# Attention in a hybrid block: sixteen small folds and divisions per launch replaced by four large ones

## The reference, cut to what matters

```python
scores = jnp.einsum('bhqd,bhkd->bhqk', q, k) * SCALE + add_mask
attn = jax.nn.softmax(scores, axis=-1)
out = jnp.einsum('bhqk,bhkd->bhqd', attn, v)
out = out.transpose(0, 2, 1, 3).reshape(b, n, H * HD)
return out @ Wo.T + bo
```

## Time and profile before

| | |
|---|---|
| time, median of 3 runs | 570.11 us (568.11 to 571.6) |
| profiled execution, first to last instruction (the page has no other time for it) | 597.5 us |
| attention loop in the profiled execution (first to last weighing) | 43.7 to 219.6 us |
| busy: PE, DVE, ACT, POOL | 82%, 72%, 56%, 44% of the span |
| 128x64 products of `weighed_T` | 128 records, 19.3 us together |

### The profile page before, as it was taken

One profiled execution on the slowest core, in us unless ns is written; L12 is line 12 of the kernel. 1 busy time (PEld: TensorE's weight loads), 2 busy tenths in 40 slices (PEclk: granted clock), 3 DMA queues, 4 the chain that ended last, 5 costly groups with the idle time before them and its releaser, 6 DMA issues.

```text
span 597.5 us, 14116 instructions
## 1 busy us (share of the span) xinstructions
PE 488.9 (82%) x4941; PEld 319.0 (53%) x4943; DVE 431.1 (72%) x1154; ACT 332.1 (56%) x509; POOL 265.0 (44%) x242
## 2 busy tenths in 40 slices
PE   7778879986999878689998887779989958879840
PEld 2435447554656545335687775225555536768730
DVE  5658896787898977566387774798988753767746
ACT  1337556554778752546377774246857823757730
POOL 5409970027000033776155556383356760645550
PEclk9999998997999998788998999978999978989985
DMA  4893642442432380111478661999001015786616
GB/s 121 203 414 88 167 111 57 123 111 67 109 98 55 101 248 2 41 50 45 130 236 251 199 194 42 238 181 150 20 19 35 29 45 157 214 251 192 187 42 210
DMA packets 85738, 78.16 MB, mean 131 GB/s; under 512 B 9645, under 2 KB 72518, under 8 KB 85286
## 3 DMA queue, kind: packets, MB, share of 16 engines
q1 hardware_dynamic: 76208, 57.81, 38.0%
q0 software_dynamic: 4544, 9.38, 4.6%
q10 hardware_dynamic: 4918, 10.07, 4.6%
HBM read 39.92 MB, written 30.88 MB: 119 GB/s over the span
## 4 chain that ended last, share of the span: by engine, by line
PE 45%; DVE 24%; ACT 9%; another core or an unknown queue 7%; issue 6%; DMA 5%; POOL 2%; SPq 2%; DVEq 0%; ACTq 0%; POOLq 0%
PE ps L1608 6%; DVE max_words L1870 5%; PE ps L1622 4%; PE ps L1361 4%; PE ps L1482 3%; PE ps L1336 3%; PE ps L1373 3%; PE ps L1285 2%; PE ps L1623 2%; ACT arena L1149 2%; ACT probs L948 2%; PE ps L1305 2%; PE ps L1559 2%; DMA arena<-y_dram 2%
## 5 line engine op out<-in xcount | busy, mean ns | idle before, releaser
L876 POOL DMA_INDIRECT y_dram<-arena,goes_to x78 | 83.5, 1071 | 91.8 <-DVE goes_to L2119 69.8
L1870 DVE TENSOR_REDUCE max_words<-ps 128x2 f32<-128x256 f32 (+3 forms) x128 | 98.6, 818 | 28.3 <-PE ps L1310 28.1
L948 ACT ACTIVATE probs<-ps 128x768 f32<-128x768 f32 (+1 forms) x96 | 81.1, 881 | 44.7 <-PE ps L1341 44.5
L727 POOL TENSOR_TENSOR rstd<-var_eps,minus_half 128x4 f32<-128x4 f32 x16 | 17.5, 1091 | 144.4 <-DVE var_eps L1837 144.4
L1149 ACT ACTIVATE arena<-ps,up_back 128x512 f32<-128x512 f32 x78 | 53.0, 679 | 48.7 <-PE ps L1608 23.3
L867 POOL DMA_INDIRECT rows_dram<-probs,idx x64 | 66.0, 1031 | 27.6 <-issue 18.0
L1608 PE MATMUL ps<-arena 128*128 128x128 f16 x936 | 65.9, 221 | 11.4 <-DVE arena L2125 11.4
L1622 PE MATMUL ps<-w,probs 128*128 x312 | 62.3, 278 | 14.3 <-DVE probs L2131 10.4
L2131 DVE SCALAR_TENSOR_TENSOR probs<-arena,hid_scale,probs 128x512 f16<-128x512 f32 x78 | 58.3, 747 | 12.8 <-ACT probs L1154 8.5
L1608 PEld LDWEIGHTS ps<-arena 128*128 128x128 f16 x936 | 56.1, 99 | 14.0 <-issue 13.7
L1482 PE MATMUL ps<-w,ident_f 128*128 128x512 f16 x184 | 53.1, 406 | 10.0 <-ACT arena L1105 3.4
(11 more groups left out here) (231 smaller groups left out, 1006.8 us busy)
## 6 DMA issues: line engine op xcount, KB each, us to landing
arena<-weights_dram SPq DMA_DIRECT2D x78, 256.0 KB
rows_dram<-grids SPq DMA_DIRECT2D x64, 260.0 KB, 4.4
heads_arena<-q_words SPq DMA_DIRECT2D x45, 128.0 KB, 2.5
qk_sb<-rows_dram SPq DMA_DIRECT2D x78, 65.0 KB
arena<-in_w ACTq DMA_DIRECT2D x2, 2304.0 KB
weights_dram<-w SPq DMA_DIRECT2D x2, 1152.0 KB, 8.4
w<-in_last_w ACTq DMA_DIRECT2D x1, 2048.0 KB, 19.2
arena<-y_dram SPq DMA_DIRECT2D x16, 128.0 KB, 4.5
```

Of the source, the lines that this page charges most:

```text
L876: nc.gpsimd.indirect_dma_start(y_dram.ap(), bass.IndirectOffsetOnAxis(ap=goes_to[:, n % AT_GO:n % AT_GO + 1], axis=0), y_t[:, n % YT, :], ...
L948: nc.scalar.activation(probs[:, n % 2, :, PROB_AT[u]:PROB_AT[u] + size], ps[:, of:of + 2, 0:size], ACT.Exp).then_inc(slot_free[slot_of(("T ...
L1870: ins = nc.vector.tensor_reduce(max_words[:, n % 2, :, t], ps[:, of:of + 2, o:o + keys], AX.X, ALU.max)
```

## The change

`weighed` gets four copies, one per quad of a batch (`weighed_of`, on words of other tiles that are idle then), so PE no longer folds each quad. Once per batch `fold_values` multiplies all four at once: `fold` is now the stationary operand, 32 columns wide, and the four quads go to the four groups of 32 columns of the array and so to the four quarters of the partitions. It does so twice, once for the numerators (first bank of the slot `at`) and once for the sums, repeated eight times so that they stand under the numerators (second bank). The result already stands as features by tokens. DVE's `divide` is called once per batch: a reciprocal of 128x512 and a product of 128x512 straight into `attT`; DVE now frees the slot `at`. The transposes, ACT's copy, `att` and the semaphores `sums_full` and `sums_free` go away. The order of the eight banks in `RINGS["all"]` changes.

```diff
-RINGS = {"all": (1, 3, 5, 7, 6, 0, 2, 4), "y": (0, 1), "wide": (2, 3, 4), "rest": (5, 6, 7)}
+RINGS = {"all": (1, 5, 0, 7, 6, 2, 3, 4), "y": (0, 1), "wide": (2, 3, 4), "rest": (5, 6, 7)}
...
+        weighed_of = [weighed[:], q_words[:, 3584:3584 + L], *(qk_sb[:, 2 * i:2 * i + 2, :].rearrange("p t d -> p (t d)") for i in range(2))]
...
             def take_weighed(g):
                 act.wait_ge(pv_made, 2 * g + 2)
-                nc.scalar.copy(weighed[:], ps[:, PV_BANK, :]).then_inc(weighed_ready, 1)
+                if g >= Q and g % Q == 0:
+                    before = ("at", g // Q - 1)
+                    act.wait_ge(slot_full[slot_of(before)], filled(before))
+                nc.scalar.copy(weighed_of[g % Q], ps[:, PV_BANK, :]).then_inc(weighed_ready, 1)
...
-            def post_tokens(a):
-                of = take(("at", a))
-                nc.scalar.copy(attT[:], ps[:, of, :]).then_inc(slot_free[slot_of(("at", a))], 1)
...
                 if n >= 2:
                     pe.wait_ge(max_copied, n - 1)
-                if n >= 4:
-                    pe.wait_ge(sums_free, (n - 2) // 2)
...
-            def weighed_T(g):
-                if g >= 1:
-                    pe.wait_ge(sums_free, g)
-                pe.wait_ge(max_copied, min(2 * g + 4, PAIRS))
-                pe.wait_ge(weighed_ready, g + 1)
-                for t in range(TT):
-                    mm = pe.matmul(sums_at(t * Q * VW, (t + 1) * Q * VW), weighed[:, t * P:(t + 1) * P], fold[:], start=True, stop=True,
-                                   skip_group_check=True)
-                mm.then_inc(sums_full, 1)
-
-            def post_tokens(a):
+            def fold_values(a):
+
                 to = give(("at", a))
-                pe.wait_ge(sums_free, 4 * a + 4)
-                for t in range(TT):
-                    mm = pe.transpose(ps[:, to, t * P:(t + 1) * P], att[:, t, :], ident[:])
+                pe.wait_ge(weighed_ready, Q * (a + 1))
+                for k in range(2):
+                    for g in range(Q):
+                        mm = pe.matmul(ps[OW * g:OW * (g + 1), to + k, :], fold[:, OW * k:OW * (k + 1)], weighed_of[g], start=True, stop=True,
+                                       skip_group_check=True)
                 mm.then_inc(slot_full[slot_of(("at", a))], 1)
...
                 scores_T(n, 1)
-                if n >= 2 and n % 2 == 0:
-                    weighed_T(n // 2 - 1)
                 scores_T(n, 2)
                 if a >= 1 and p == 1:
-                    post_tokens(a - 1)
+                    fold_values(a - 1)
...
             tokens_T(0, 0)
-            weighed_T(QUADS - 1)
+            fold_values(B - 1)
             tokens_T(0, 1)
             gates(0, 0)
-            post_tokens(B - 1)
             tokens_T(0, 2)
...
-            pe.wait_ge(sums_free, QUADS)
+            read_by(("at", B - 1))
             gates(0, 2)
-            read_by(("at", B - 1))
             ranks(0, 0)
...
-            def divide(g):
-                a, q = divmod(g, 4)
-                dve.wait_ge(sums_full, g + 1)
-                if q == 0 and a >= 1:
-                    dve.wait_ge(slot_full[slot_of(("at", a - 1))], filled(("at", a - 1)))
-                sums = sums_at(0, TT * Q * VW).rearrange("p (t h w) -> p t h w", t=TT, h=Q)
-                core_link(nc.vector.reciprocal(rec[:], sums[:, :, :, HD]))
-                nc.vector.tensor_tensor(att[:, :, Q * q * HD:Q * (q + 1) * HD].rearrange("p t (h d) -> p t h d", h=Q),
-                                        sums[:, :, :, 0:HD], rec[:].unsqueeze(3).broadcast_to([P, TT, Q, HD]),
-                                        ALU.mult).then_inc(sums_free, 1)
+            def divide(a):
+
+                of = take(("at", a))
+                if a >= 1:
+                    before = ("wo", a - 1)
+                    dve.wait_ge(slot_full[slot_of(before)], filled(before))
+                core_link(nc.vector.reciprocal(rec[:], ps[:, of + 1, :]))
+                nc.vector.tensor_tensor(attT[:], ps[:, of, :], rec[:], ALU.mult).then_inc(slot_free[slot_of(("at", a))], 1)
...
-                if n >= 2 and n % 2 == 0:
-                    divide(n // 2 - 1)
+                if a >= 1 and p == 1:
+                    divide(a - 1)
                 if a >= 1 and p == 2:
                     attention_post(a - 1)
...
-            divide(QUADS - 1)
+            divide(B - 1)
             tokens_split(0)
```

More of the change, by code:

```diff
@@ L319, in hybrid_block_kernel @@
         cos, sin = (k_words[:, L * i:L * (i + 1)] for i in range(2))
+        weighed = sb("weighed", [P, L])
+        weighed_of = [weighed[:], q_words[:, 3584:3584 + L], *(qk_sb[:, 2 * i:2 * i + 2, :].rearrange("p t d -> p (t d)") for i in range(2))]
         max_words = sb("max_words", [P, 2, 2, TT])
@@ L324, in hybrid_block_kernel @@
         v_tok = v_flat[:, 0:2 * TT * HP * VS].rearrange("p (a t g w) -> p a t g w", a=2, t=TT, g=HP)
-        fold = sb("fold", [P, Q * VW])
+        fold = sb("fold", [P, 2 * OW])
         heads_arena = sb("heads_arena", [P, 8192])
@@ L330, in hybrid_block_kernel @@
         probs = sb("probs", [P, 2, 2, PROBS])
-        weighed = sb("weighed", [P, L])
-        rec = sb("rec", [P, TT, Q])
-        att = sb("att", [P, TT, D])
+        rec = sb("rec", [P, L])
         attT = sb("attT", [P, L])
@@ L404, in hybrid_block_kernel @@
         hid16_t = part(probs_words, 2048, [HT, 2, F], F16)
-        routeT = att[:].rearrange("p t d -> p (t d)")[0:X, :]
+        routeT = rec[0:X, :]
         routeT4 = q_words[0:X, 0:B * L].rearrange("p (a l) -> p a l", a=B)
@@ L469, in hybrid_block_kernel @@
         weighed_ready = sem("weighed_ready")
-        sums_full = sem("sums_full")
-        sums_free = sem("sums_free")
         bias_added = sem("bias_added")
@@ L584, in max_columns @@
             return ps[0:4 * TT, Q2_BANK, (n % 2) * (P // 2):(n % 2 + 1) * (P // 2)].bitcast(BF16)
-        def sums_at(start, end):
-            return ps[:, Q2_BANK, L // 2 + start:L // 2 + end]
         @block.sync
@@ L1027, in _ @@
                 exps(n, 2)
-                if a >= 1 and p == 1:
-                    post_tokens(a - 1)
                 if n in XN_IN:
@@ L2319, in halves @@
         return np.tile(a.reshape(2, W2, P).transpose(1, 0, 2), (2, 1, 1)).astype(mybir.dt.np(BF16))
+    fold = np.zeros((2, 2, 2, VW, 2, Q, HD), np.float32)
+    for q in range(2):
+        for h in range(2):
+            fold[:, h, q, 0:HD, 0, 2 * q + h, :] = np.eye(HD)
+            fold[:, h, q, HD, 1, 2 * q + h, :] = 1.0
     later = np.arange(P)[None, :] > np.arange(P)[:, None]
@@ L2335, in shape_constants @@
         "cos": table(cos), "sin": table(sin),
-        "fold": np.tile(np.eye(Q * VW, dtype=np.float32).reshape(2, 2, VW, Q * VW).transpose(1, 0, 2, 3).reshape(Q * VW, Q * VW), (2, 1)),
+        "fold": fold.reshape(P, 2 * OW),
         "ident": np.eye(P, dtype=np.float32),
```

## The result

The changed kernel takes 579.71 us (median of four runs, 574.15 to 583.28) against 569.11 for the kernel before (566.23 to 571.60): 10.6 us more, a ratio of 1.0145 with a 95% interval of 1.009 to 1.0201. The prediction was 577, in a range of 563 to 587. Medians are of all runs; ratios and their intervals leave out runs more than 1.5% above the fastest of their kernel. The profiled execution of the changed kernel took 578.56 us (span 576.6), so it stands for the median without any carrying over.

A forecast was written before the change was run, and what follows sets the result against it. In the attention loop neither DVE (41.28 of 46.5 us busy) nor PE (38.85) had much room. Costs 18.2 + 0.8 less 12 saved gave 7 us more; 570.1 + 7 = 577 us, range 563 to 587.

The forecast's parts named there:

- the gain: Attention loop: 15 quad folds go from PE, worth 14.5 us; DVE takes part back, so 12 us saved.
- The reciprocal: DVE, once per batch: a reciprocal of 128x512 takes 3.3 us, between bounds of 0.69 and 3.8.
- The rivals of a cheap and of a dearer reciprocal: DVE's division: reciprocal like a product, 0.69 us, total 564 (chance 0.15); or dearer, total 579 to 581 (0.10).
- The fold of a batch: PE, replacing the transposes: eight fp32 products over four column groups side by side, 2.0 us, 1.35 us more.
- the serial rival: PE's batch fold: column groups go one after another, 5.9 us more three times, total 595; chance 0.04.
- nine beats: Loop beats with projections or turning of tokens: PE works without pause, so each removed fold gives 1.0 us, 9.0 together.
- DVE's load: First loop stretch: DVE has 39.1 us to do, PE would offer about 41.5, cutting 14.5 saved to 12.
- The rival of the small gain: Loop: DVE or ACT closes the beats, only 7 us are kept, total 582; chance 0.13.
- DVE's stand: Beats 9, 17, 25: division delays the next maxima and holds PE's slot, 14.3 us plus 3.9 for slow clock: 18.2.
- the 3.9 added for the clock: After the stands of beats 9, 17 and 25: PE's slow clock costs 1.3 us three times.
- The rival of the absorbed stand: Loop: slow clock does not follow and the whole 14.5 us is kept, total 571, no change; chance 0.22.
- Behind the loop: After the loop: the last batch's division ends 3.5 us later, 1.1 come through, PE gains the transposes: 0.8 us more.

The follow-up runs named there:

- the constant: Changed kernel with its four 128x512 reciprocals replaced by a same-size DVE operation writing a constant, so the output lacks the division: 565.8 us, 0.9917 of the kernel before.
- the second execution of the kernel before: The kernel before, unchanged, profiled once more: 568.49 us.
- the kernel where ACT scales: Changed kernel without DVE's division of the first three batches; ACT copies the numerators times a constant into attT: 567.42 us, 0.9942 of the kernel before.
- The lump from SBUF: Changed kernel, but ACT copies numerators and sums out of PSUM, DVE divides all 512 columns from SBUF at once, projection later: 583.86 us, 1.0249.
- The two moves: Kernel before with the bounds moved from turn 15 to 14 and batch 3's measures from turn 7 to 8: 558.54 us, 0.9807.

## Why the prediction was right

The sign, the mechanism and the place were right; the sum of 7 us came out at 10.6. One term, the gain, was 4.5 us too large, and two smaller errors the other way, 2.2 us together, hid half of that: so far the nearness of 577 to 579.71 is luck.

- **The reciprocal**: 3.3 us taken, 3.35 measured. From 4 elements (167 ns) to 512 (3353) an element costs 6.3 ns, between the two readings of the earlier trace rows. The Trainium skill, "VectorE: DVE Perf Modes", section "First, the fixed hardware budget", gives the count of eight repeats and no time for one; the prediction's estimate from it, at a product's column for each, was 8.3 ns an element and 4.4 us. The measurement differs from that estimate, and it decides. The rivals of a cheap and of a dearer reciprocal fall.
- **The fold of a batch**: 2.0 taken, 1.9 measured. The groups ran side by side; the serial rival falls.
- **The gain: 12 taken, 7.5 measured.** This is the step that failed, as to size: "In nine beats with projections or with the turning of tokens PE works without a pause, and it is 1.0." With the constant, all beats but 9, 17, 25 and 26 give 7.5 us against the second execution of the kernel before. The nine beats (2, 4, 6, 10, 12, 14, 18, 26 and 28; 26 from the kernel where ACT scales) give 4.0 us together, not 9.0: 0.8 in beats 14 and 28, and 0.2 to 0.4 in the others. In beats 2, 4, 10, 12 and 18 PE now stands 0.46 to 0.77 us for ACT's exponentials, where in the kernel before it stood for nothing of ACT's. The other terms were about right: 0.38 us each in beats 20, 22 and 24 for 0.43, and 2.1 and 1.7 in beats 8 and 16 for 1.95. What was put down to DVE's load, 2.5, came as 1.4, and from elsewhere: beats 7 and 15 are 0.8 and 0.6 longer, since PE waits 1.31 and 0.63 us there for the split of the maxima, which took 2.02 and 0.98 us beside POOL (in the kernel before 1.32 and 0.50, with 0.9 us of waits in all). Beat 8 took 10.03 us in one execution of the kernel before and 11.36 in the other, so single beats there are uncertain by that much. The rival of the small gain had 7, and it named ACT among the engines that would close the beats.
- **DVE's stand: 18.2 taken, 16.8 measured**: 5.3 us in beats 9, 17, 25 and 26 that stay with the constant (folds, products, less what the removed folds gave in beat 26), and 11.5 for 3 x 2.66 = 8.0 us of reciprocal. DVE's wait for the fold, 1.74, 1.66 and 1.74 us, was foreseen at 1.75. PE's stands for the product, 2.62, 2.62 and 2.20 us, are at the low end of the 2.5 to 4 or below it. The clock fell behind two of them (0.75 and 0.83), not three. The 3.5 us above DVE's 8.0 are close to the 3.9 added for the clock, but beat 9, behind which the clock stayed at 1.00, grew by 3.8 us for 2.66 too, so how much of them is clock is not shown. The rival of the absorbed stand falls.
- **Which of DVE's links holds PE**: the prediction named both the late maxima and the slot. The lump from SBUF shows that the late maxima are enough: its loop takes 182.6 us with no slot held, the changed kernel's 182.9.
- **Behind the loop**: 0.8 taken; from the last weighing to the addition to x the changed kernel takes 15.2 us and the kernel before 15.4, so nothing. (With the constant it is 13.5: the last reciprocal does cost 1.7, and the rest of the change gives as much back.) The bank order has no price, as said. What is left of the 10.6 us, 1.3, lies behind that and stays open: from that addition to the end, four profiled executions with the old end of attention took 331.7 to 334.5 us (the first one, of 597.5, left out), and the changed kernel with its eight variants 335.0 to 339.3, so a cost there is possible; the bank order alone is not it (331.7).

The gain was 4.5 us too large, the stand 1.4, the tail 0.8: 7 - 0.8 - 1.4 + 4.5 = 9.3, what the loop lost.

## What to carry to other kernels

Count a division by the elements that each partition divides: sums repeated eight times to suit the layout made 512 of them a batch where 64 had done, and the engine that paid (DVE) was not the one that was relieved (PE). An instruction that goes counts only down to the next wait at its place, so look there before pricing it at its length. And where DVE's operations on a few columns take 2 us, look at what POOL is doing beside them: moving two such pieces by one turn gave the kernel before 11.2 us, about what the change cost.

## What the runs showed that was not expected

- A DVE operation on one column in SBUF with two inputs took 2.38 us beside POOL and 0.15 away from it, and the profile lists no wait for it. One-column operations with one input took 0.14 beside POOL, and maxima read from PSUM took 3.17 us for four, much as elsewhere (3.0 to 3.2).
- The two moves were worth 11.2 us of 570 (569.75 to 558.54), 8.7 of them in the loop, where the stands of beats 8 and 16 and the slow clock behind them went away.
- A logarithm and an exponential on ACT cost two table loads of 1.28 us in each of the three batches.
